# A graph attention layer on one core: q and VectorE's V weights read from PSUM, the last sum taken a stage sooner

## What is computed

```python
def _sparse_attention(z, row, col, bias, Wq, bq, Wk, bk, Wv, bv, Wo, bo):
    q = (z @ Wq + bq).reshape(L, H, D)
    k = (z @ Wk + bk).reshape(L, H, D)
    v = (z @ Wv + bv).reshape(L, H, D)
    scale = 1.0 / jnp.sqrt(jnp.asarray(D, z.dtype))
    scores = jnp.einsum('ehd,ehd->eh', q[row], k[col]) * scale + bias
    m = jax.ops.segment_max(scores, row, num_segments=L)
    p = jnp.exp(scores - m[row])
    ssum = jax.ops.segment_sum(p, row, num_segments=L)
    alpha = p / ssum[row]
    out = jax.ops.segment_sum(alpha[:, :, None] * v[col], row, num_segments=L)
    return out.reshape(L, C) @ Wo + bo
...
x = x + att
z = _ln(x, ln2_g, ln2_b)
ff = jax.nn.silu(z @ W1 + b1) @ W2 + b2
return x + ff
...
x = _layernorm(x + _L0_gnn_ref(...), axis=-1)
```

## Time and profile before

| | us |
|---|---|
| median of 3 runs | 3755.35 |
| lowest, highest | 3748.81, 3761.47 |
| the profiled execution | 3755.59 |
| its span | 3753.8 |
| PE busy | 2858.6 (76%) |
| VectorE busy | 2618.3 (70%) |
| ACT busy | 1714.6 (46%) |
| POOL busy | 2692.9 (72%) |

### The profile page before, as it was taken

The page is one execution under the profiler, slowest core; times in us unless marked ns, Lnnn a source line. Parts: engine busy times, 40 slices in busy tenths (PEclk is TensorE's granted clock), DMA queues, the critical chain, the costliest instruction groups (busy, mean ns, idle before and its releaser), DMA issues.

```text
span 3753.8 us, 82235 instructions
## 1 busy us (share of the span) xinstructions
PE 2858.6 (76%) x18693; PEld 2193.6 (58%) x18694; DVE 2618.3 (70%) x6428; ACT 1714.6 (46%) x6427; POOL 2692.9 (72%) x2550
## 2 busy tenths in 40 slices
PE   8566566666665663777888888888888898889897
PEld 6333333333333332666767777777777777777776
DVE  9676667676766674556767777777777777777775
ACT  0111111111111111556667676676766666767664
POOL 0377777777777776777777777777777777777771
PEclk9977666766776676788999999999999999999999
DMA  7322322232223224676887788878787878788771
GB/s 269 89 76 76 90 79 75 77 90 79 76 76 90 79 74 138 223 249 220 279 284 270 253 278 279 275 265 292 235 283 263 282 256 288 254 280 262 266 252 43
DMA packets 285667, 719.24 MB, mean 192 GB/s; under 512 B 86899, under 2 KB 103475, under 8 KB 285382
## 3 DMA queue, kind: packets, MB, share of 16 engines
q0 software_dynamic: 211776, 585.54, 47.2%
q1 hardware_dynamic: 73862, 133.41, 11.2%
HBM read 717.02 MB, written 72.97 MB: 210 GB/s over the span
## 4 chain that ended last, share of the span: by engine, by line
POOL 36%; issue 36%; DMA 7%; PE 7%; POOLq 5%; DVE 5%; ACT 2%; DVEq 1%; ACTq 0%; PEld 0%; SPq 0%; PEldq 0%
POOL region_a L522 18%; POOL records L409 16%; DMA records<-region_c,pos_i 5%; PE bank L1221 2%; PE bank L1322 2%; DVE region_c L939 1%; ACT region_c L704 1%; DMA out_dram<-region_c,out_idx 1%; PE wide L1380 1%; POOL cols L500 1%; PE bank L1390 1%; POOLq L522 1%; DVE region_c L904 1%; DVE pos_i L922 0%; POOLq L390 0%
## 5 line engine op out<-in xcount | busy, mean ns | idle before, releaser
L522 POOL DMA_INDIRECT region_a<-kv,cols x1160 | 1474.7, 1271 | 415.2 <-issue 368.0
L409 POOL DMA_INDIRECT records<-region_c,pos_i x1024 | 1010.9, 987 | 460.9 <-issue 291.5
L704 ACT ACTIVATE region_c<-region_a,pr 128x64 f32 x4640 | 1155.8, 337 | 33.4 <-issue 33.3
L992 DVE TENSOR_TENSOR region_c<-region_a,region_c 128x1024 f32 x580 | 676.9, 1221 | 233.8 <-SPq L367 127.6
L1322 PE MATMUL bank<-ident,region_c 128*128 128x128 f32 x4640 | 642.4, 297 | 218.7 <-DVE region_c L992 218.5
L1322 PEld LDWEIGHTS bank<-ident,region_c 128*128 128x128 f32 x4640 | 605.5, 199 | 255.3 <-issue 220.9
L1340 PE MATMUL wide<-ident,region_c 128*128 128x128 f32 x4640 | 571.6, 277 | 76.2 <-ACT region_c L704 76.2
L1340 PEld LDWEIGHTS wide<-ident,region_c 128*128 128x128 f32 x4640 | 520.2, 145 | 109.4 <-ACT region_c L704 109.4
L627 ACT COPY region_c<-region_a 128x64 f32 x128 | 32.5, 254 | 1033.0 <-DMA records<-region_c,pos_i 1033.0
L1279 PE MATMUL bank<-region_b,region_a 128*128 128x512 f32 x768 | 487.0, 793 | 0.0
L1266 PE MATMUL wide<-region_c 64*128 64x64 f32 x2048 | 193.5, 345 | 207.0 <-issue 189.0
(11 more groups left out here) (184 smaller groups left out, 3241.9 us busy)
## 6 DMA issues: line engine op xcount, KB each, us to landing
region_a<-srcT SPq DMA_DIRECT2D x128, 256.0 KB
region_a<-kv,cols POOLq DMA_INDIRECT x1160, 5.9
region_a<-hiT SPq DMA_DIRECT2D x256, 64.0 KB
x_rows<-region_c SPq DMA_DIRECT2D x32, 512.0 KB, 3.4
records<-region_c,pos_i POOLq DMA_INDIRECT x1024
kv<-region_a SPq DMA_DIRECT2D x32, 512.0 KB
records<-region_c SPq DMA_DIRECT2D x32, 480.0 KB, 14.7
region_a<-in_x_dram SPq DMA_DIRECT2D x32, 256.0 KB
```

The costliest lines, as they stand in the source:

```text
L409: pool.indirect_dma_start(records, bass.IndirectOffsetOnAxis(ap=pos_i[j % 2][:, s:s + 1], axis=0), rec_w[j % 2][:, s, :], None).then_inc(S ...
L522: pool.indirect_dma_start(KV[r][:, s, :], None, kv, bass.IndirectOffsetOnAxis(ap=cols[r][:, s:s + 1], axis=0), bounds_check=L - 1, oob_is_ ...
L704: last = act.activation(vw[:, s, of], v_part[:, s, C + hd * D:C + (hd + 1) * D], ACT.Copy, scale=pr[:, s + 1, hd:hd + 1])
L992: last = dve.tensor_tensor(prods[:, of, :], kv_in[:, of, 0:C], q.unsqueeze(1).broadcast_to([P, 2, C]), ALU.mult)
```

## The change

A tile's q is copied once, in stage 0, from SBUF into PSUM bank 3, and all products read it there. ACT computes the exponents of VectorE's four slots a second time, straight into PSUM bank 4, and `weigh` on VectorE reads them there. To free the two banks, `wo_ps` moves into bank 2, where tiles are turned, and `y_ps` into bank 5, which holds the first half of the hidden layer. So `y_ps` must be read before the next `up` writes that bank: the addition leaves `last_norm` in stage 2 and becomes `take_y` in stage 1, and PE's wait for it moves from `down` to `up`.

```diff
--- before.py
+++ after.py
@@ -214,8 +214,9 @@
         qkv_ps = [bank[3], bank[4], bank[3]]
         scT_ps, sc_ps = bank[0][:, 0:2 * P], bank[0][:, 2 * P:2 * P + 2 * SH]
         vT_ps, acc_ps = bank[1], bank[7]
-        wo_ps, y_ps = bank[3], bank[4]
+        wo_ps, q_ps = turn_ps, bank[3]
         h_ps = bank[5:7]
+        y_ps, pv_ps = h_ps[0], bank[4][:, 0:(GROUP - 4) * HEADS].rearrange("p (s h) -> p s h", h=HEADS)
 
         names = """kv00 kv01 kv02 kv03 kv10 kv11 kv12 kv13 kv20 kv21 kv22 kv23 more_loaded rec_loaded src_loaded edges_loaded weights_loaded consts_a pad_ready
             table_cleared bias_cut bias_out bias_in hist_in hist_turned keys_ready turned turned_sb turned_out onehots_free onehots_ready hist_done prefix_in
@@ -685,6 +686,7 @@
             def exponents():
 
                 act.wait_ge(S["sc_ready"], now)
+                act.activation(pv_ps, sc[:, 3:GROUP - 1, :], ACT.Exp)
                 act.activation(pr[:, 0:GROUP + 1, :], sc[:, :, :], ACT.Exp).then_inc(S["p_ready"], 1)
                 act.drain()
 
@@ -983,14 +985,13 @@
 
             def products():
 
-                q = row_q[:, bass.ds(dve.snap(q_at, min_val=0, max_val=C), C)]
                 kv_in = slots(at)
                 dve.wait_ge(S["scT_ready"], groups)
                 for pair in range(PAIRS):
                     of = slice(2 * pair, 2 * pair + 2)
                     dve.wait_ge(LANDED[pair], now)
                     last = dve.tensor_tensor(prods[:, of, :], kv_in[:, of, 0:C],
-                                             q.unsqueeze(1).broadcast_to([P, 2, C]), ALU.mult)
+                                             q_ps[:, :].unsqueeze(1).broadcast_to([P, 2, C]), ALU.mult)
                     if pair % 2:
                         last.then_inc(PRODS[pair // 2], 1)
 
@@ -1002,7 +1003,7 @@
                     dve.wait_ge(SUMMED[s // 2], groups)
                     dve.tensor_tensor(vw[:, s:s + 2, :].rearrange("p s (h d) -> p s h d", h=HEADS),
                                       kv_in[:, s:s + 2, C:2 * C].rearrange("p s (h d) -> p s h d", h=HEADS),
-                                      pr[:, s + 1:s + 3, :].unsqueeze(3).broadcast_to([P, 2, HEADS, D]),
+                                      pv_ps[:, s - 2:s, :].unsqueeze(3).broadcast_to([P, 2, HEADS, D]),
                                       ALU.mult).then_inc(V_READY[s // 2], 1)
 
             def scale():
@@ -1052,11 +1053,14 @@
             def summed(reg):
                 return s_all[:, bass.ds(dve.snap(reg, min_val=0, max_val=C), C)]
 
-            def last_norm(k, u, s_w):
+            def take_y(k, s_w):
 
                 dve.wait_ge(S["y_done"], k + 1)
                 dve.tensor_tensor(s_w, s_w, y_ps[:, :], ALU.add).then_inc(S["y_taken"], 1)
                 dve.drain()
+
+            def last_norm(u, s_w):
+
                 dve.bn_stats(stats[:, :], s_w)
                 dve.drain()
                 dve.bn_aggr(mv[:, 2:4], stats[:, :])
@@ -1101,6 +1105,8 @@
             def body(t, stage):
                 if stage == 0:
                     hold(S["q_loaded"], t * 16 + 16)
+                    dve.tensor_copy(q_ps[:, :], row_q[:, bass.ds(dve.snap(q_at, min_val=0, max_val=C), C)])
+                    dve.drain()
                 products()
                 if stage == 0:
                     with dve.If(t > 0):
@@ -1116,6 +1122,8 @@
                     weigh()
                     dve.tensor_copy(sc[:, 0, :], m_run[:, :])
                 if stage == 1:
+                    with dve.If(t > 2):
+                        take_y(dve.snap(oldest), summed(dve.snap(dve.snap(q_at) * -1 + C)))
                     with dve.If(t > 0):
                         finish(t)
                     first_weights()
@@ -1160,7 +1168,7 @@
                 if stage == 2:
                     with dve.If(t > 2):
                         other = dve.snap(dve.snap(q_at) * -1 + C)
-                        last_norm(dve.snap(oldest), bass.ds(dve.snap(nc.s_assert_within(t - 3, 0, NT - 4, skip_runtime_bounds_check_because="the If has t > 2")), 1),
+                        last_norm(bass.ds(dve.snap(nc.s_assert_within(t - 3, 0, NT - 4, skip_runtime_bounds_check_because="the If has t > 2")), 1),
                                   summed(other))
                     dve.nop()
 
@@ -1186,19 +1194,22 @@
             middle(NT - 1)
             hold(S["out_sent"], 16 * (NT - 3))
             residual(half(NT - 2))
+            take_y(NT - 2, half(NT - 3))
             dve.reg_add(groups, groups, 1)
             finish(NT)
             silu(NT - 1, 0)
-            last_norm(NT - 2, slice(NT - 3, NT - 2), half(NT - 3))
+            last_norm(slice(NT - 3, NT - 2), half(NT - 3))
             silu(NT - 1, 1)
             middle(NT)
             hold(S["out_sent"], 16 * (NT - 2))
             residual(half(NT - 1))
-            last_norm(NT - 1, slice(NT - 2, NT - 1), half(NT - 2))
+            take_y(NT - 1, half(NT - 2))
+            last_norm(slice(NT - 2, NT - 1), half(NT - 2))
             silu(NT, 0)
             silu(NT, 1)
             hold(S["out_sent"], 16 * (NT - 1))
-            last_norm(NT, slice(NT - 1, NT), half(NT - 1))
+            take_y(NT, half(NT - 1))
+            last_norm(slice(NT - 1, NT), half(NT - 1))
 
         @block.tensor
         def _(pe):
@@ -1375,6 +1386,7 @@
 
                 if a == 0:
                     pe.wait_ge(S["z2_sb"], k)
+                    pe.wait_ge(S["y_taken"], k)
                 for m in range(a * HT // 2, (a + 1) * HT // 2):
                     for c in range(KT):
                         last = pe.matmul(h_ps[m // 4][:, (m % 4) * P:(m % 4 + 1) * P], W1_sb[:, c, m * P:(m + 1) * P],
@@ -1384,8 +1396,6 @@
             def down(k, a):
 
                 pe.wait_ge(H_READY[a], k)
-                if a == 0:
-                    pe.wait_ge(S["y_taken"], k)
                 for m in range(a * HT // 2, (a + 1) * HT // 2):
                     last = pe.matmul(y_ps[:, :], hT[:, m * P:(m + 1) * P], W2_sb[:, m, :], start=m == 0, stop=m == HT - 1)
                 if a == 1:
```

## The result

| | before | after |
|---|---|---|
| median, in the comparison | 3752.39 us (4 runs, 3748.81 to 3761.47) | 3632.82 us (4 runs, 3631.54 to 3641.99) |
| ratio, 95% interval | | 0.9683 (0.9659 to 0.9708) |
| profiled execution | 3755.59 us | 3641.99 us |
| its span | 3753.8 us | 3640.2 us |
| VectorE's wait for the output row block | 105.9 us | gone |

3632.8 us against 3636 forecast, inside 3600 to 3685. The changed kernel was timed once more beside the last experiments: 3636.1 us, ratio 0.9687.

A forecast was written before the change was run, and what follows sets the result against it. POOL's gathers, slowed by VectorE's two-SBUF-operand instructions, were taken to set the pace. Savings of 35 + 49 + 36 + 3 - 4 = 119 us from 3755.6 gave 3636 us, range 3600 to 3685.

The forecast's parts named there:

- The bound and the gathers: POOL's row gathers, slowed beside two-SBUF-operand VectorE instructions, lose 326.3 us; freed, their mean falls to about 1.00 us.
- PSUM operands at no cost: VectorE's products and V weights with one operand in PSUM take no longer; products stay at 1.22 us.
- Rivals 2 and 4: Rival 2: PSUM surcharge of 65 ns, 3657 us, chance 0.14. Rival 4: broadcast PSUM operand at half pace, 4180, chance 0.05.
- rival 3: The change doesn't free POOL's gathers, so its pace stays: 3750 to 3762 us; chance 0.07.
- POOL's pace reaches VectorE as the wait for the output: VectorE's 105.9 us wait for the output row block is how POOL's pace holds it, 3.8 us a tile.
- two thirds of the saving return as POOL's waiting: Of the 326 us POOL is given, two thirds come back as its waiting for free buffers.
- The copy at 1.0 us, uncovered: Copy of q and drain before a tile's first products, hidden by nothing: 1.0 us a tile, bounds 0.6 to 1.1.
- The sum moved, y_taken, wo and the tail at nothing: take_y a group earlier, PE's y_taken wait at up, wo in turn_ps: 0 us; y_taken's bounds -2 to +5.
- The four-group tile: 56.9 us free, plus 1.0 copy, 0.7 clock, 0.1: 58.7 us, saving 2.3 each, 35 us over 15 tiles.
- The five-group tile: 67.5 us free, plus 1.0 copy, 1.0 clock, 0.4: 69.9 us, saving 4.1 each, 49 us over 12 tiles.
- Rival 1: Lighter: TensorE's clock does not fall and the copy costs 0.6 us: 36 us more saved, 3600 us; chance 0.14.
- The first three tiles: They follow POOL: 19 groups x 2.25 = 43 us, of which 36 taken; 4 us deducted for one remaining output wait.

The follow-up runs named there:

- send_early3: Kernel before, with POOL sending a finished output block after a tile's first group instead of its second; third chip: 3738.5 us, ratio 0.9951.
- copy_twice3: Changed kernel with the copy of q into PSUM and its drain done twice in each tile; third chip: 3670.08 us.
- q_late3: Changed kernel with the next tile's q copied in a tile's last group, between products and maximum; third chip: 3620.62 us, ratio 0.9643.
- q_plain: Kernel before with q alone in PSUM, V weights from SBUF, the last sum still in stage 2: 3640.61 us, ratio 0.9692.
- q_only: Changed kernel with VectorE's V weights read from SBUF again and no second exponent; q stays in PSUM: 3641.31 us, ratio 0.9695.
- after, second run: The changed kernel itself, unaltered, timed again on a third chip beside the last experiments: 3636.1 us, ratio 0.9687.

## Why the prediction held

- **The bound and the gathers: right.** L522's mean of 1.271 us fell to 1.001 (said: about 1.00), and the dose of 0, 2, 4 and 6 instructions gives 12, 59 to 76, 209 and 326 to 334 us. The rule of the Trainium skill in "SBUF — State Buffer", "Who interferes with whom", that a VectorE instruction with two SBUF inputs contends with GpSimd's reads and one with a single SBUF input does not, agrees with this. Its inference that tensor_tensor would not stall the generation of descriptors is contradicted by these kernels.
- **PSUM operands at no cost: right.** 1217 ns against 1221, also for the broadcast operand of 1024 that no row had shown. The Trainium skill's fixed cost in "VectorE: DVE Perf Modes", "The TRN2 errata", 120 cycles with PSUM sources against 58 with SBUF sources, would make the PSUM form the longer one; it is not. Rivals 2 and 4 fall with it, rival 3 with the gathers.
- **POOL's pace reaches VectorE as the wait for the output: right**, by send_early3 above. That two thirds of the saving return as POOL's waiting: 222.6 of 339.8 us came back as idle time, 133.9 of them named as waits for buffers, where some 200 were said.
- **The copy at 1.0 us, uncovered: nearly.** 0.87 us by copy_twice3, and uncovered, except that 0.7 us of it could be hidden in four-group tiles by another place (q_late3).
- **The sum moved, y_taken, wo and the tail at nothing: right** where the chain is the bound (q_plain against q_only). While POOL is the bound the moved sum makes the kernel 18 us slower, which I had not seen; in the change nothing is left of it.
- **The four-group tile: right**, 58.7 us said and 58.7 measured, saved 35.2 (said 35). A tile without a slowed clock took 58.07 us (said 58.0), and the clock took 0.6 us a tile (said 0.7): 5 of these 15 tiles were slowed, at 1.5 to 2.8 us each, where half were said, at 1.5.
- **The five-group tile: the step that was mis-sized.** 69.9 us said, 71.1 measured, saved 35.3 instead of 49. Without a clock drop such a tile is 15.66 + 11.21 + 17.69 + 11.65 + 12.62 = 68.8 us, intervals of after by their shortest or usual value, and 67.5 + 1.0 + 0.4 = 68.9 was said. The clock was charged 1.0 us and took 2.3. I had it fall in two thirds of the tiles at 1.5 us; in fact the first interval is 0.5 to 2.3 us over 15.66 in all twelve, and the third 0.4 to 0.7 over 17.69. The 1.5 us priced the first 16 turnings alone. In the tile from 2102.34 us these take 3.65 us at a granted clock of 0.50, and the next 16 still 2.64 us, at 0.73, instead of 1.97. In the second and third intervals of that tile the granted clock is 1.00, but PE has come late: its turnings for the second group begin 4.10 us behind that group's first product, 3.64 in an unslowed four-group tile, and the third interval pays for that. Rival 1, for which the clock does not fall, falls here.
- **The first three tiles: low.** 41.6 us saved, 36 less 4 said; the transfers left more room than I gave them, and no output wait stayed. This (10 us more) makes up for most of the five-group tiles (14 less): 113.6 us in sum by the trace, 119 said. So the nearness of 3632.8 to 3636 us is in part luck: two misses of opposite sign, and a profiled execution 9 us longer than the median.

The clock at a tile's first turnings, from PE's timeline of after, first in a tile behind a five-group tile, then in one behind a four-group tile:

```profile
1821.42 3.65 PE L1333 MATMUL bank<-ident,region_c 128*128 128x128 f32 x16 [2.55 <-DVE region_c L993]
...
2897.48 2.04 PE L1333 MATMUL bank<-ident,region_c 128*128 128x128 f32 x16 [1.82 <-DVE region_c L993]
```

The same row of before and then of copy_twice3, each in a tile behind a four-group tile:

```profile
2921.75 2.04 PE L1322 MATMUL bank<-ident,region_c 128*128 128x128 f32 x16 [0.99 <-DVE region_c L992]
```

```profile
2668.00 2.04 PE L1335 MATMUL bank<-ident,region_c 128*128 128x128 f32 x16 [2.70 <-DVE region_c L993]
```

The stretches inside the two rows of after (PEclk is the third value from the end):

```profile
1822.00:1824.30 2.30, 2.30 (x13) 2.30 (x12) 2.30 (x3) 0.94 (x4) 1.82 (x4) 0.50 0.88 306
2898.00:2899.50 1.50, 1.50 (x16) 1.50 (x15) 1.50 (x2) 1.50 (x8) 1.20 (x2) 1.00 0.80 289
```

PE idles 2.5 us before the first turnings behind a five-group tile, because VectorE comes late to that tile's end (the maximum ahead of 1821.42 begins 0.81 us after its scores were there, the one ahead of 2897.48 only 0.17), and 1.82 us behind a four-group tile. The granted clock was 0.50 (the 1.2 GHz level) after the first of these pauses and 1.00 (2.4 GHz) after the second. The first turnings of tiles 4 to 15, all behind a five-group tile, and of tiles 16 to 30, behind a four-group tile, were slowed this often:

| kernel | idle before tiles 4-15, us | slowed | idle before tiles 16-30, us | slowed |
|---|---|---|---|---|
| before | 1.9 to 2.2 | 5 of 12 | 1.0 to 1.1 | 0 of 15 |
| after | 2.5 to 2.6 | 12 of 12 | 1.8 | 5 of 15 (16, 22, 23, 29 and 30) |
| after, second run | 2.5 to 2.6 | 12 of 12 | 1.8 | 1 of 15 |
| copy_twice3 | 3.4 | 12 of 12 | 2.7 | 9 of 15 |
| q_late3 | 2.4 to 2.5 | 11 of 12 | 1.0 to 1.2 | 0 of 15 |

So a longer pause is slowed more often, but its length alone does not decide: 2.7 us behind a four-group tile of copy_twice3 were slowed in 9 of 15, 2.5 us behind a five-group tile of after in all. I had read the pause of the kernel before from a tile behind a five-group one, 1.92 us, and taken it for both kinds; behind a four-group tile it was 0.99.

## What to carry to other kernels

Count the instructions that read two SBUF operands beside a queue of GpSimd's gathers, and price their collisions from two rows of the same trace; a PSUM operand took the price away at no cost to VectorE. But the gain ends where the next chain takes over: here half of the operands in PSUM brought as much as all of them, and what the move adds at a place where all engines wait (one copy a tile) cost as much as the other half gained. Before charging or hiding such a step, ask in each kind of tile which engine is the late one there. And measure on more than one chip: on the second chip three relatives of the changed kernel were 1.4 to 2.5% slower than before, though their gathers were as free as on the first.

## What was not expected of the hardware

- A chip on which the same program takes 16% more (4370 against 3755 us) and the order of versions is reversed, with gathers, products and V weights as long as on the first, and with engines standing still for no reason that the profile knows.
- How TensorE's clock answered a pause that grew by less than 1 us: behind four-group tiles no first turnings of 15 were slowed at 1.0 us of idle, 5 and 1 at 1.8, 9 at 2.7; behind five-group tiles 5 of 12 at 1.9, all at 2.5.
- Taking the sum sooner, neutral with freed gathers, costs 18 us with held ones.
